# First attention's row maxima at a lead of 24 heads instead of 28, with the two passes through the shared PSUM bank exchanged

## The reference, cut to what matters

```python
q = jnp.einsum('oc,bct->bot', Wq, x) + bq[None, :, None]
k = jnp.einsum('oc,bct->bot', Wk, c) + bk[None, :, None]
v = jnp.einsum('oc,bct->bot', Wv, c) + bv[None, :, None]
scores = jnp.einsum('bhkt,bhks->bhts', q, k) * SCALE
p = jax.nn.softmax(scores, axis=-1)
out = jnp.einsum('bhts,bhks->bhkt', p, v)
```

## Time and profile before

| | |
|---|---|
| median of 3 runs | 777.53 us (777.05 to 778.8) |
| the profiled execution's own time | 779.62 us |
| its span, first to last instruction | 777.4 us |
| PE busy | 667.8 us, 86% |
| DVE busy | 531.6 us, 68% |
| ACT busy | 379.0 us, 49% |
| share of PE in the chain that ended last | 56%, DVE 13% |

### The profile page before, as it was taken

How to read it: one execution, slowest core, us unless ns; L and a number is a source line. 1 busy time by engine, 2 the same in 40 slices (tenths; PEclk the granted TensorE clock), 3 DMA queues, 4 the chain that set the end, 5 groups by cost and what they waited for, 6 DMA issues and landing times.

```text
span 777.4 us, 13620 instructions
## 1 busy us (share of the span) xinstructions
PE 667.8 (86%) x4737; PEld 349.5 (45%) x4738; DVE 531.6 (68%) x1252; ACT 379.0 (49%) x630; POOL 324.1 (42%) x337
## 2 busy tenths in 40 slices
PE   3889999999999899688735788999977999888996
PEld 1233333333333367576402244444433476555763
DVE  3889888888895699155278899997736743222336
ACT  2057888878787344244314566676502213333320
POOL 3535353535011101753568878831100057666530
PEclk9999999999999999889956999999979999999999
DMA  6834343444311800446447778896530022222137
GB/s 164 176 92 122 97 113 96 135 140 130 106 33 38 265 13 2 121 138 184 125 116 190 185 185 205 209 217 158 140 110 28 1 57 83 72 75 66 56 97 258
DMA packets 106362, 93.23 MB, mean 120 GB/s; under 512 B 25205, under 2 KB 92954, under 8 KB 106104
## 3 DMA queue, kind: packets, MB, share of 16 engines
q1 hardware_dynamic: 93600, 67.67, 32.5%
q0 software_dynamic: 8352, 18.74, 8.9%
q10 hardware_dynamic: 4344, 5.97, 2.9%
HBM read 50.63 MB, written 16.01 MB: 86 GB/s over the span
## 4 chain that ended last, share of the span: by engine, by line
PE 56%; DVE 13%; issue 11%; POOL 9%; DMA 4%; ACT 2%; SPq 2%; another core or an unknown queue 1%; ACTq 0%; POOLq 0%; DVEq 0%
PE O L447 9%; PE S L404 9%; PE ST L1547 6%; POOL spare L268 6%; DVE mx L566 4%; PE ST L1473 2%; PE S L1564 2%; PE M L1564 2%; PE ST L943 2%; POOL QKc L279 2%; PE ST L412 2%; PE M L496 2%; DMA QS<-mxT 2%; SPq L165 2%; PE M L489 1%
## 5 line engine op out<-in xcount | busy, mean ns | idle before, releaser
L566 DVE TENSOR_REDUCE mx<-S 128x2 f32<-128x512 f32 x384 | 250.7, 684 | 35.8 <-PE S L404 33.9
L319 ACT ACTIVATE PX<-ST 128x1024 f32<-128x1024 f32 x192 | 195.8, 1022 | 88.2 <-PE ST L412 79.2
L404 PE MATMUL S<-QS 62*128 62x256 bf16 (+1 forms) x768 | 151.2, 292 | 41.6 <-DVE mx L566 28.4
L412 PE MATMUL ST<-QS 64*128 64x256 bf16 (+1 forms) x768 | 141.0, 278 | 7.3 <-DMA QS<-mxT 7.3
L447 PE MATMUL O<-PX,VA 128*32 128x256 f32 x1536 | 123.3, 394 | 0.1
L404 PEld LDWEIGHTS S<-QS 62*128 62x128 bf16 (+1 forms) x768 | 48.7, 97 | 158.2 <-DVE mx L566 95.7
L268 POOL DMA_INDIRECT spare<-ye,GI x64 | 68.9, 1077 | 30.4 <-DMA ye<-QKc 16.1
L1658 POOL DMA_INDIRECT PX<-xn,TI x39 | 39.9, 1022 | 63.4 <-DVE K1n L1847 39.7
L412 PEld LDWEIGHTS ST<-QS 64*128 64x128 bf16 (+1 forms) x768 | 53.4, 96 | 23.3 <-DMA QS<-mxT 9.8
L1547 PE MATMUL ST<-EGU,Cb 128*128 x156 | 54.2, 471 | 6.3 <-ACT Cb L1615 4.9
L786 POOL DMA_INDIRECT PX<-xn,TI x32 | 33.5, 1046 | 61.2 <-DVE spare L1183 44.1
(11 more groups left out here) (302 smaller groups left out, 1114.2 us busy)
## 6 DMA issues: line engine op xcount, KB each, us to landing
QS<-QKs SPq DMA_DIRECT2D x177, 128.0 KB
EGU<-in_ew SPq DMA_DIRECT2D x16, 256.0 KB, 2.8
xn<-spare SPq DMA_DIRECT2D x8, 512.0 KB, 5.7
ye<-QKc SPq DMA_DIRECT2D x32, 128.0 KB
VA<-in_val SPq DMA_DIRECT2D x16, 256.0 KB
spare<-yt SPq DMA_DIRECT2D x16, 256.0 KB, 6.3
Cb<-in_ctx SPq DMA_DIRECT2D x31, 128.0 KB
on<-OS SPq DMA_DIRECT2D x27, 128.0 KB
```

The lines of the kernel that those rows point to most:

```text
L319: e.activation(M["PX"][pair % 4][:, :], M["ST"][pair % 2][:, :], ACT.Exp, scale=A.scale).then_inc(A.exp, 1)
L404: got = e.matmul(M["S"][n % 2][:, 256 * a:256 * a + 256], QS[:, 0, 128 * a:128 * a + 128], QS[:, 1, :], start=True, stop=True)
L412: got = e.matmul(M["ST"][(NP * t + k // 2) % 2][:, 512 * u + 256 * a:512 * u + 256 * a + 256], QS[:, 1, 128 * a:128 * a + 128], QS[:, 0, : ...
L566: e.tensor_reduce(M["mx"][b % 2][:, :, A.row_of_max(head)], M["S"][n % 2][:, :].rearrange("p (a s) -> p a s", a=2), AX.X, ALU.max, negate= ...
```

## The change

The lead becomes 24 heads. In PE's order `context` stands after `k = 5` and `maxima` after `k = 9`. ACT copies the transposed maxima after pair `m = 4` instead of 2, and DVE adds the bias of the values after its maximum `k = 6` instead of 10. The operations and their number stay the same.

```diff
-        self.lead = H + 12 if self.first else H + 6
+        self.lead = H + 8 if self.first else H + 6
...
-                if m == 2 and within(b2):
+                if m == 4 and within(b2):
                     rows_out(b2)
...
                 if k == 5 and within(b2):
-                    maxima(b2)
+                    context(b2)
                 if k in (6, 7, 10, 11, 14, 15) and within(b3):
                     values(b3, k // 4 - 1, k % 2)
                 if k == 9 and within(b2):
-                    context(b2)
+                    maxima(b2)
...
-                if k == 10 and within(b2):
+                if k == 6 and within(b2):
                     w.wait_ge(A.vt, b2 + 1)
```

## The result

| | kernel before | changed kernel |
|---|---|---|
| median | 777.29 us (776.73 to 778.8, 4 runs) | 787.3 us (782.63 to 793.45, 4 runs) |
| ratio | | 1.0125, 95% interval 1.0082 to 1.0168 |
| profiled execution | 779.62 us (taken beside the four), span 777.4 | 789.02 us (one of the four), span 787.0 |

The account below looks back on a forecast made before the run. PE sets the pace of settled steps with DVE close behind; before the first exponential PE only feeds DVE. The terms -2.8 (start), +1.8 (steps) and +2.9 (step 14) gave +1.9, so 779.4 us, range 776.0 to 781.8.

Parts of the forecast that it names:

- term C: Step 14: DVE's next-network block between k = 5 and k = 6 makes PE wait 2.7 us before transposes; +2.9 us.
- The stall lowers the clock: Rival: step 14's 2.7 us wait brings 3.4 us at half rate, up to 1.7 us more; 781.1 us, chance 0.10.
- Term A: The start: 24 heads instead of 28 pass before the first exponential, 0.695 us of DVE each; -2.8 us.
- Term B: Steps 0 to 13: a 0.18 us wait goes, a 0.32 one comes at k = 9; +0.13 each, +1.8 us.
- The transfers: Shifted rows and context loads in the steps: nothing lost, but close; SP issues the rows at 130.3 us.
- zero, with 0.1 us left: Context load in the steps: at most 3.3 us, landed by 149.1 for its reader at 149.2, so no cost.
- this rival: A late transfer makes PE wait for rows or context, 0.2 us in each of 12 steps; 781.8 us, chance 0.08.

Follow-up runs that it names:

- e5: The changed kernel again without any edit, on the chip of the second group: ratio 1.0103 (1.0056 to 1.0150) to the kernel before.
- e10: The changed kernel with only the next step's context load issued ahead of the shifted rows: ratio 1.0102 (1.0055 to 1.0149) to the kernel before.
- e12: The changed kernel with 22 needless products on PE in place of its idle time in step 14: ratio 1.0033 (0.9997 to 1.0070) to the kernel before.
- e3: The kernel before, with PE's transposes of batch 15 in step 14 also waiting for DVE's first statistics (2.44 us): ratio 1.0100 (1.0061 to 1.0138).
- e8: The kernel before, with PE's transposes in dense step 8 also waiting about 2 us for POOL's third piece of work: ratio 1.0055 (1.0023 to 1.0086).
- e9: The changed kernel, context load first, DVE's next-network work spread over steps 14 and 15 behind what PE needs: ratio 1.0002 (0.9973 to 1.0032) to the kernel before.
- e11: The kernel before, batch 15's transposes waiting only for the first statistics themselves (1.82 us): ratio 1.0020 (0.9982 to 1.0057) without the two longest of twelve, 1.0031 with all.
- e6: The kernel before again without any edit, on the chip of the second group: ratio 1.0006 (0.9969 to 1.0044).
- e2: The changed kernel's new order with the lead kept at 28 heads as in the kernel before: ratio 1.0049 (1.0021 to 1.0078) to the kernel before.
- e4: The changed kernel, step 14's constants and first statistics after k = 7, context load ahead of shifted rows: ratio 1.0020 (0.9993 to 1.0046) to the kernel before.
- e1: The changed kernel with step 14's constants and first statistics on DVE after k = 7 instead of k = 5: ratio 1.0048 (1.0017 to 1.0079) to the kernel before.
- e7: The changed kernel, statistics after k = 7, context load first, first normalized rows at k = 14 of step 14: median of twelve 759.5 us, 10 above the kernel before.

## Why the prediction was wrong

The sign was right and the size was not: +1.9 us forecast, +10 measured, outside the range. With the clock in the sum the forecast would have been 1.9 + 4.3 = +6.2 us. That is close to the medians of the two later groups (7.6 us in e5, 6.5 in e10), and still under the 10 of the first comparison.

**The step that failed** is the clock behind the stall of term C, which the sum put at nothing and left to the rival "The stall lowers the clock", in the prediction's words "3.4 us of work at half rate cost up to 1.7 us more", with a chance of 0.10. It was no rival but what the stall of term C does: in all three profiles of the changed order with the block in its place (the change, e5, e10) the clock is at its lower level for 10.2 us right behind the wait. It costs 4.3 us by e12. The length was taken from one window, the 3.40 us from 260.60. That fall, soon behind the end of the first attention, is itself one of single executions: it stands in 5 of 14 profiles (the kernel before, e3, e8, e9, e11) and is missing in the other profile of the kernel before, e6. The length should have been bounded by the longest stretch. The clock row of the profile of the kernel before, in 40 slices of 19.4 us, shows longer ones further on:

```profile
PEclk9999999999999999889956999999979999999999
```

Its windows read 0.51 from 325.30 for 10.2 us and 0.50 from 390.40 for 30.4 us. That idle time of PE is the cause is shown from both sides: a wait alone brings it (e3, e8), and products in the wait's place prevent it (e12). Why it stays down for 10 us and not 3.4 is open.

**Term C**, +2.9 us, was right: the wait forecast at 2.7 us measured 2.60 (2.59 and 2.60 in e5 and e10), and the step's delay without the clock 2.95.

**Term A**, -2.8 us, was right: -2.68 at line 472 of step 0, and 40.09 to 40.54 in the nine profiles with lead 24 against 43.17 to 43.38 in the five with lead 28. Line 412 first ran at 39.41, where 39.1 was forecast. Of the 2.2 us that came back in step 0 of this profile the prediction had about 1 as a bound; it was taken for a property of the change and is one of single executions, of either lead (e2, e6).

**Term B**, +0.13 us a step, was about twice too large: 132.93 us for ten steps in e10 and 132.94 in e4 against 132.29, 0.065 each. The wait before `k = 9` was right. The view gives it as 0.18 us because it counts from the modelled end of `k = 8`; against the 0.28 us in which one bare head follows another it is 0.30 (127.95 + 0.28 to 128.53), 0.32 forecast. What was mis-sized is the old wait that goes. The prediction took 0.38 for the transposes and 0.18 for the wait behind them; with no wait behind them the next head starts 0.32 after the transposes (128.86 to 129.18), so the old wait was worth 0.24 us and the balance is about 0.06 a step. Over 14 steps that is 0.9 us and not 1.8.

**The transfers.** SP issues the rows at 130.29, as forecast at 130.3, and PE never waits for them. The context's "zero, with 0.1 us left" failed by its thin margin. The chain of waits of the changed kernel shows the issue in step 8 and the landing, for which step 9 waits:

```profile
158.60 4.54 DMA Cb<-in_ctx
163.18 0.70 PE M L474 x2
```

4.54 us instead of at most 3.3. SP issued the next spreads at 160.29, while this transfer was under way; that they slowed it is likely and not shown. 133.72 - 132.93 = 0.8 us in this profile, 2.1 in e5. So this rival came true in the profiles, in two steps and not in twelve; in the times of e10 its removal does not show.

The sum in the profile up to line 496 of step 15: -2.7 at the start, +2.2 by chance in step 0, +1.4 in ten steps (0.65 the order, 0.8 contexts), +0.1 in steps 11 to 13, +7.2 in steps 14 and 15, together +8.3 with rounding. The 1.3 us behind the first attention were not traced one by one. They look like a balance: at line 866 the difference is down from 8.33 to 6.67 us (264.10 against 270.77), behind the fall of the clock at 260.60 that only the kernel before has there, and from 262 us on the two profiles spend about 68 and 76 us at the lower clock, in different places. Nor is it settled why the times of the changed kernel scatter over 11 us beside 2 us of the kernel before: in the first two groups the kernel before scattered over 8 to 9 us too, in the third over 15 us (770.8 to 786.3, three of 935 us and more left out), and the change over 5.5 us in e5. So the scatter is not a mark of the change. On the chip of the second group the change measures 1.0103, so about 2 us of the 10 may belong to the first comparison alone; the intervals overlap.

## What to carry to other kernels

A pipeline's lead also sets where its last work ends, so look at what stands behind the old end on the same in-order engine; here one block of 2.5 us came to stand before two small reductions that PE needed. Price a wait of about 2 us on TensorE as the wait and the clock behind it, and take the clock's stretch from the longest that the trace shows, not the nearest. Where the wait can't be removed, cheap products in its place are worth trying: in the profiles here they gave back 4.3 of 7.2 us.

## What the runs showed that was not expected

- In the first attention a wait of 1.8 to 2.6 us on PE had the lower clock in its last part or soon behind it (within 0.7 us, in e11 after 1.9) in seven profiles of seven (the change, e3, e5, e7, e8, e10, e11). The clock stayed low for 3.4 us in a dense step (e8) and 3.4 to 17.1 us in steps 14 and 15, where PE has no products for maxima, although PE was then busy nearly all the time. In the profiles of e1 and e4 waits of 1.14 and 1.15 us left it up.
- The Trainium skill, "TensorE: Matmul & The Clock Gate", section "HAM oscillation — how this bites in real kernels", warns of idle gaps. The runs agree on the effect; the gaps that sufficed here were 1.8 to 2.6 us long, shorter than those the section warns of.
- In step 0 the granted clock reads 1.00 in every window, yet eight values products take 1.08 us in some executions and 0.64 in others. Before the first recorded change the duration of a known product tells the clock, not the column.
